# Last batch of an attention kernel: weight loads of the head behind the early gathers, value-weight splits on VectorE, first query tile ahead of the second's transposes

## What is computed

```python
x = x + xattn(layernorm(x), ctx)      # 16 heads of 32; text keys (118) and image keys (257),
                                      # each with its own softmax, the two outputs added, then @ o_w
h = layernorm(x)
score = h @ w_router                  # per token
idx = sort(top_k(score, 14))          # 14 tokens of every batch: 448 in all
sel = h[b, idx]
q, k, v = rms(sel) @ wq + bq, rms(sel) @ wk + bk, rms(sel) @ wv + bv   # 16 query, 8 key/value heads of 128
x1  = sel + causal_attention(rope(q), rope(k), v) @ wo
mlp = (silu(rms(x1) @ w_gate) * (rms(x1) @ w_up)) @ w_down
x = x + h.at[b, idx].set(gate * (x1 + mlp) + (1 - gate) * sel)        # gate = sigmoid(score)
```

## Time and profile before

| | us |
|---|---|
| median of 3 runs | 1636.01 (1633.88 to 1638.73) |
| the profiled execution | 1640.35, its span 1638.6 |
| PE (TensorE matmuls) busy | 1572.6, 96% of the span |
| DVE (VectorE) | 1195.5, 73% |
| ACT (ScalarE) | 708.7, 43% |
| POOL (GpSimd) | 703.5, 43% |
| DMA engines, mean over the span | 69 GB/s |

### The profile page before, as it was taken

One profiled execution on the slowest core, in us unless ns is written; L12 is line 12 of the kernel. 1 busy time (PEld: TensorE's weight loads), 2 busy tenths in 40 slices (PEclk: granted clock), 3 DMA queues, 4 the chain that ended last, 5 costly groups with the idle time before them and its releaser, 6 DMA issues.

```text
span 1638.6 us, 42293 instructions
## 1 busy us (share of the span) xinstructions
PE 1572.6 (96%) x16778; PEld 1219.5 (74%) x16778; DVE 1195.5 (73%) x1872; ACT 708.7 (43%) x1461; POOL 703.5 (43%) x781
## 2 busy tenths in 40 slices
PE   6999999999999999999999999999986999998997
PEld 5776777777777777777777777777765786777996
DVE  5753788877887788887888878788776685544775
ACT  5763444434444444444444444444434114555331
POOL 6761444344343444434444344443435581113552
PEclk9999999999999999999999999999996998999998
DMA  5842111112111121111211112111135223010000
GB/s 182 243 141 72 45 54 53 47 60 71 51 52 47 54 74 53 52 47 50 75 56 52 47 49 75 58 52 47 47 103 207 72 105 153 28 50 27 1 0 23
DMA packets 66167, 113.71 MB, mean 69 GB/s; under 512 B 21392, under 2 KB 36080, under 8 KB 64576
## 3 DMA queue, kind: packets, MB, share of 16 engines
q1 hardware_dynamic: 65280, 110.20, 21.4%
q0 software_dynamic: 832, 2.75, 0.5%
HBM read 82.59 MB, written 30.34 MB: 69 GB/s over the span
## 4 chain that ended last, share of the span: by engine, by line
PE 88%; ACT 5%; DVE 3%; DMA 2%; POOL 1%; issue 1%; SPq 0%; DVEq 0%; ACTq 0%; POOLq 0%
PE ps L1409 21%; PE ps L1410 18%; PE ps L1411 18%; PE ps L1539 7%; PE ps L1514 7%; PE ps L1487 3%; PE ps L1461 3%; PE ps L1724 2%; PE ps L1741 2%; ACT prob L770 2%; PE ps L1517 2%; PE ps L1733 1%; DMA xh_sel<-xh_dram,tok 1%; ACT prob L768 1%; PE ps L1443 1%
## 5 line engine op out<-in xcount | busy, mean ns | idle before, releaser
L490 POOL TENSOR_TENSOR ctx_lo<-ctx_raw,ctx_hi 128x472 fp32r<-128x472 f32 x64 | 115.4, 1827 | 310.6 <-ACT ctx_hi L711 310.6
L527 POOL TENSOR_TENSOR prob_img<-prob 128x448 f32<-128x448 f32 x128 | 160.3, 1253 | 189.2 <-ACT prob L770 189.1
L1075 DVE RECIPROCAL rec<-ps 128x224 f32<-128x224 f32 x128 | 199.0, 1555 | 6.8 <-PE ps L1539 3.2
L768 ACT ACTIVATE prob<-ps 119x448 f32<-119x448 f32 x128 | 69.7, 545 | 205.5 <-PE ps L1517 205.5
L1514 PEld LDWEIGHTS ps<-q_all,k_all 32*128 32x128 f32 (+1 forms) x3072 | 121.7, 186 | 49.3 <-issue 31.4
L1514 PE MATMUL ps<-q_all,k_all 32*128 32x112 f32 (+1 forms) x3072 | 148.3, 301 | 10.0 <-ACT prob L770 10.0
L1064 DVE TENSOR_REDUCE top<-ps 112x4 f32<-112x1028 f32 x128 | 156.2, 1221 | 0.0
L744 ACT ACTIVATE sq_junk<-proj 128x513 bf16<-128x513 f32 (+1 forms) x96 | 61.1, 637 | 172.5 <-DVE proj L1043 172.5
L1063 DVE TENSOR_REDUCE top<-ps 112x4 f32<-112x472 f32 x128 | 83.0, 649 | 65.8 <-PE ps L1487 65.8
L1069 DVE SCALAR_TENSOR_TENSOR prob_img<-prob,ones_last,prob_img 23x448 f32<-23x448 f32 x128 | 93.1, 727 | 42.6 <-POOL prob_img L527 39.5
L770 ACT ACTIVATE prob<-ps 128x896 f32<-128x896 f32 x128 | 116.9, 914 | 0.0
(11 more groups left out here) (326 smaller groups left out, 4421.3 us busy)
## 6 DMA issues: line engine op xcount, KB each, us to landing
ctx_raw<-in_ctx_dram SPq DMA_DIRECT2D x32, 748.0 KB, 4.2
xh_dram<-xh SPq DMA_DIRECT2D x32, 448.0 KB, 3.1
q_dram<-q_turned SPq DMA_DIRECT2D x28, 256.0 KB, 2.8
q_all<-q_dram SPq DMA_DIRECT2D x32, 224.0 KB, 3.1
xh<-in_x_dram SPq DMA_DIRECT2D x32, 224.0 KB
out_dram<-out_sb SPq DMA_DIRECT2D x32, 224.0 KB, 2.3
xa<-in_x_dram SPq DMA_DIRECT2D x21, 256.0 KB, 3.6
ring<-in_wq_dram SPq DMA_DIRECT2D x1, 4096.0 KB, 19.4
```

The costliest lines, as they stand in the source:

```text
L490: nc.gpsimd.tensor_tensor(ctx_lo[:, :, cols], ctx_raw[:, :, cols], ctx_hi[:, :, cols].bitcast(F32), ALU.subtract).then_inc(ctx_lo_done, 1)
L527: nc.gpsimd.tensor_tensor(prob_img[:, g % 2], prob[:, g % 2, 1, :], prob[:, g % 2, 2, :], ALU.add).then_inc(img_summed, 1)
L1075: nc.vector.reciprocal(rec[:], bank[:, 2:4]).then_inc(norm_step, 1)
```

## The change

Five edits:

1. SP, `last`: before the load of wq it waits for the three early gathers to have landed.
2. GpSimd, `last`: the three gathers are issued in one go right after `normalise_h(p)`, ahead of `output(p)` and `sum_image(i, 0)`. Three of the four value-weight splits leave GpSimd; the fourth (half 1, part 1) stays at the end and waits for all `oT_lo` parts of batch 31.
3. ScalarE, `last`: both `value_weights_hi` move up, from between the exponentials to just after `value_text(i)`, ahead of `turn_top(i, 0)`. VectorE, `last`: splits (0, 0), (0, 1) and (1, 0) run right after `score(p)`.
4. GpSimd behind the batches: `weights_lo(2)` waits until the normalised fourth chunk is written.
5. TensorE, prologue: `queries(0)` runs before `turn_x(1)`; from tile 1 on the order is as before.

```diff
@@ sync, last
                 sp.dma_start(xh[:, 0], t["x"][bass.ds(i, 1)].rearrange("o t d -> t (o d)")).then_inc(xres_loaded, 16)
+                for c in range(EARLY):
+                    sp.wait_ge(gathered[c], 16)
                 sp.dma_start(wq, t["wq"].rearrange("(c p) n -> p c n", p=P)).then_inc(ring_loaded[0], 16)
@@ gpsimd, last
                 normalise_h(p)
-                output(p)
                 pool.wait_ge(tok_ready, 1)
                 pool.wait_ge(xh_stored, 16 * EARLY_B)
                 pool.wait_ge(scaled, 3 * i + 3)
                 pool.wait_ge(k_tail_done, i + 1)
-                gather(0)
+                for c in range(EARLY):
+                    gather(c)
+                output(p)
                 sum_image(i, 0)
-                gather(1)
-                gather(2)
-                value_weights_lo(0, 0)
                 sum_image(i, 1)
-                value_weights_lo(0, 1)
                 sum_image(i, 2)
                 token_roots(slice(0, EARLY), 1)
                 sum_image(i, 3)
                 residual(i)
-                value_weights_lo(1, 0)
-                value_weights_lo(1, 1)
+                pool.wait_ge(oT_lo_done, B - 1 + KC)
+                at = (slice(None), slice(2, 4), slice(512, 1024))
+                nc.gpsimd.tensor_tensor(wv_lo[at], wv[at], wv_hi[at].bitcast(F32), ALU.subtract).then_inc(w_lo_done, 1)
@@ gpsimd, behind the batches
             token_roots(slice(EARLY, NC), 2)
+            pool.wait_ge(normed_ready, NC)
             weights_lo(2)
@@ scalar, last
                 value_text(i)
+                value_weights_hi(0)
+                value_weights_hi(1)
                 turn_top(i, 0)
                 turn_top(i, 1)
                 exps(i, 0)
-                value_weights_hi(0)
                 exps(i, 1)
-                value_weights_hi(1)
                 token_squares(0)
@@ vector, last
+            def value_weights_lo(half, part):
+                dve.wait_ge(w_hi_done, half + 1)
+                at = (slice(None), slice(2 * part, 2 * part + 2), slice(512 * half, 512 * half + 512))
+                return nc.vector.tensor_tensor(wv_lo[at], wv[at], wv_hi[at].bitcast(F32), ALU.subtract)
+
                 score(p)
+                value_weights_lo(0, 0)
+                value_weights_lo(0, 1)
+                value_weights_lo(1, 0).then_inc(w_lo_done, 1)
                 add_tail(i, 0)
@@ tensor, pre
                 turn_x(0)
+                queries(0)
+                turn_x(1)
                 for k in range(NT):
-                    if k + 1 < NT:
-                        turn_x(k + 1)
-                    queries(k)
                     if k:
+                        if k + 1 < NT:
+                            turn_x(k + 1)
+                        queries(k)
                         turn_q(k - 1)
```

## The result

| | before | after |
|---|---|---|
| median, runs on one chip | 1635.34 (4 runs, 1633.88 to 1638.73) | 1625.17 (4 runs, 1624.15 to 1627.08) |
| ratio, 95% interval | | 0.9936 [0.9918, 0.9955] |
| profiled execution | 1640.35, span 1638.6 | 1627.08, span 1625.3 |

The kernel is 10.2 us faster by medians and 13.3 us by spans; the forecast was 1622.7 in a range of 1617 to 1630. For the stages I use two quantities that need no absolute time. The **lead** is when the load of wv goes out (1213.04 before). The **stretch** runs from there to the first matmul of the head: 1290.54 - 1213.04 = 77.5 us before. After, it is 1277.21 - 1212.83 = 64.4 us. So 13.1 of the 13.3 us lie in the stretch and 0.2 in the lead.

What follows compares the result with a forecast made beforehand. TensorE matmuls, busy 96% of the span, bound the kernel, with waits in the last batch on gathers and one VectorE instruction. Gains 6.8 + 4.4 + 0.9 + 1.2 = 13.3 us off 1636.0 give 1622.7, range 1617 to 1630.

Steps and rivals of the forecast that it cites:

- Part 1: Last batch: gathers ahead of GpSimd's other work, with wq and wk loads behind them, gain 6.8 us.
- The cover of the roundings: ScalarE, last batch: moved roundings put topT(0) at 1225.0 instead of 1220.6; 0.4 us of cover, nothing on the path.
- Part 2: Last batch: moving value-weight splits off GpSimd cuts add_tail(3) from 6.29 to about 1.9 us, gain 4.4.
- Clock: TensorE: fewer gaps may keep it at 2.4 GHz in places, between nothing and 2 us; counted as nothing.
- Part 3: Behind the batches: GpSimd's wait before weights_lo(2) removes TensorE's idle time for normed_last, gain 0.9 us.
- Part 4: Prologue: running queries of x tile 0 first starts the batches earlier, gain 1.2 us, ends 0 and 2.2.
- the median is 4.3 below that execution; taken off the median: Final sum: the 13.3 us gain is subtracted from the median 1636.0, not the profiled 1640.35, giving 1622.7.
- A: Last batch: gathers and splits exclude each other, 3.3 us less gain, 1626.0 us; chance 0.15.
- B: Last batch: gathers are slow by themselves, not through wq; total gain 8.0 us, 1628.0; chance 0.06.
- C: Last batch: ScalarE's new wait for wv makes it slower than before, 1642 if wv takes 28 us; chance 0.04.
- D: Last batch and behind: wq's landing or the fourth gather holds what moved forward, half the gain, 1629; chance 0.07.

Runs made afterwards that it cites:

- e4: Kernel before with only the value-weight splits moved to VectorE and the roundings moved up; median 1636.80 us, ratio 1.0004.
- e3: Kernel before with only SP's wait for the three early gathers added ahead of wq and wk; median 1633.74 us, ratio 0.9985.
- e12: Changed kernel with all four value-weight splits back on GpSimd at their old places; median 1633.86 us, ratio 0.9975.
- e1: Kernel before with only the prologue edit, queries of x tile 0 ahead of tile 1's transposes; median 1635.35 us, ratio 1.0004.
- e6: Changed kernel without GpSimd's wait in front of weights_lo(2); median 1626.34 us, ratio 0.9932.
- e10: Changed kernel with GpSimd's old order of gathers, output and image sum, loads' wait kept; median 1625.26 us, ratio 0.9926.
- e8: e7 with residual(i) moved between the sums over images 1 and 2 on GpSimd; median 1621.21 us.
- e9: e7 with two GpSimd waits, before the batch's second image sum and before residual, that open gaps; median 1620.12 us, ratio 0.9901.
- e2: Changed kernel with the prologue's old order, without queries(0) first; median 1626.30 us, ratio 0.9942.
- e7: Changed kernel with GpSimd's first context split made in two parts, tiles 24 and 26 instead of 23; median 1622.41 us, ratio 0.9911.

## Why the prediction was right, point by point

**Part 1, right in its sum, partly by luck.** From wv's issue to exps(3) it is 27.3 us instead of 34.1: 6.8, the forecast's number. The gathers landed in 4.4 to 7.2 us (forecast 4.4 each). The terms inside were off. The forecast had exps(2) 7.4 us earlier and then 0.6 lost up to exps(3); measured are 6.2 and another 0.6 gained. Exps(2) started at 1236.46 and not 1235.3, because add_tail(0) took 1.54 us and not 0.68: I had put sum_image(0) in front of it and missed that sum_image(1) now follows without a gap and keeps VectorE out. The same 1 us came back further on: scores_T(3) started at 1238.87 and not 1238.1 (1.0 late, with the lead of 0.2), but its matmuls ran in 1.2 us instead of 2.1, at a granted clock of 1.00 instead of 0.50 (windows view, first before, then after):

```profile
1244.20:1246.50 2.30, 2.23 (x40) 2.12 (x44) 1.81 (x2) 0.21 (x2) 1.13 (x1) 0.50 1.00 367
```

```profile
1238.80:1240.10 1.30, 1.30 (x48) 1.17 (x44) 1.09 (x1) 0.00 (x0) 1.13 (x3) 1.00 0.96 391
```

The forecast had taken nothing for the clock, so two errors of 1 us cancelled. And wq went out at 1236.27 instead of 1233.8; it landed after 13.7 us, at 1250.0, within the 1253.2 of the forecast. The cover of the roundings held: topT(0) at 1224.08, wv landed after 7.6.

**Part 2, right in size; the partition between parts 1 and 2 is wrong.** From exps(3) to the end of add_tail(3) it was 8.9 us and is 4.7: 4.2, against 4.4, and e4 has the same by itself (4.3 us, a gain of 4.6). But the forecast gave the splits no other value and gave part 1 its full 6.8 by itself, and e3, e4 and e12 show otherwise. With the splits on GpSimd, shielding the gathers is worth 2.8 us (e3; e12, which has part 3 as well, comes to 2.9); with the gathers unshielded, moving the splits is worth 1.5; both together, and the 1.0 of part 3 set aside, 77.5 - 64.4 - 1.0 = 12.1. Some 8 us exist only for the pair, and nearly all of it lies ahead of exps(3): there the pair gains 6.8, while e3 gains 3.2, because VectorE is kept out, and e4 loses 3.7, because its splits hold up the gathers' issue. The times agree in kind: 2.5 us by e3's ratio, nothing by e4's, 10.5 by the changed kernel's, part 3 included. The row that shows the first half was in the trace of before, o_space with 3.16 us under the gathers' wait, and I had not priced what that wait was hiding.

**Clock.** Between the end of add_tail(3) and add_residual(31) another 1.0 us went (7.9 to 6.9). The forecast took 0 out of 0 to 2. The granted clock there was 0.50 in the earlier trace rows. In the changed kernel and, second, in e1 this stretch reads:

```profile
1244.80:1251.70 6.90, 6.30 (x72) 4.96 (x72) 6.09 (x12) 2.21 (x6) 1.21 (x1) 0.83 1.01 418
```

```profile
1255.40:1262.00 6.60, 5.99 (x30) 4.43 (x31) 5.95 (x11) 2.43 (x6) 0.00 (x0) 0.68 0.00 0
```

e1 took 6.6 us here without any edit of the last batch, so I don't count this 1.0 as the change's for certain. With the 0.9 in scores_T(3) the clock gave back 1.9 us in this one execution, the upper end of what the forecast allowed and took nothing for.

**Part 3, right.** 0.9 forecast, 1.0 in e6; normed_last 0.48 us.

**Part 4, the step that failed.** The 1.2 us were there at turn_q(0), as forecast, and are 0.2 at wv's issue, and nothing in the means over ten kernels. "Behind it the loop is again TensorE's own, so 1.0 to 1.5 stays" was wrong. TensorE waits 2.4 us at tile 23 in both kernels; the lead outlived even that, and was then spent at the lower clock. The 2.4 us stood in the trace of before; the fall of the clock did not.

**From the trace to the median.** By spans the forecast's 13.3 us is what came, with part 4 short by 1.0 and the clock's 1.0 in its place. That the sum agrees to the tenth is luck: the errors cancelled, and each span is one execution. By medians it is 10.2, inside an interval of 7.4 to 13.4 (1635.34 times 0.0045 and 0.0082). The difference is in the step "the median is 4.3 below that execution; taken off the median": the changed kernel's profiled execution stands only 1.9 above its median. In the profiled executions of these 14 kernels the part behind the first head matmul, the same program in all, took 343.5 to 348.1 us, and in before and after it happened to be the longest, 348.1 in both. Inside it, the attention stage from its first to its last maximum (neg_top on VectorE) took 126.8 to 127.7 us in seven of them, after included (127.4), and 128.4 to 129.2 in the other seven, before included (129.2); TensorE's granted clock was 0.99 over that stage in after and 0.96 in before. The part from there to the last result rows gave it back, 149.5 us in after and 147.5 in before. What decides this was not settled, and with it stays open where the 3 us between spans and medians went.

**Rivals.** A (1626.0) is nearer to the median, 1625.17, than the forecast's 1622.7 and can't be told from it by the time, but by the trace: no engine lost a whole turn. The second gather took 1.73 us beside the splits and 0.94 in e12 where VectorE was idle; the first gather of e4 and e10 took 1.96 beside a split and 1.19 in e3 without; the first gather of the changed kernel took 1.56 beside a split and 1.57 in e12 without. So splits cost a gather between nothing and 0.8 us, not its turn. By the Trainium skill, "SBUF — State Buffer", section "Who interferes with whom", arithmetic with two SBUF inputs on VectorE and a GpSimd instruction that reads SBUF block each other; the trace agrees for arithmetic. Its inference that such an instruction leaves descriptor generation alone is borne out for one of these three gathers and not quite for the other two, by 0.8 us each. B is out: 4.4 to 7.2 us of landing. C did not occur. D names something late behind the batch, and TensorE was busy 25.00 of 25 us there.

## What to carry to other kernels

Two waits that overlap hide each other: before pricing the removal of one, list every instruction in its shadow that takes longer than its usual time, since that is what will be late next. Where GpSimd and VectorE share the path, and a VectorE operation starts behind the first instruction of a GpSimd row without a gap, it is what is left of the row that counts here, not the instruction that happens to run; moving an instruction within the row moves the block, a gap ends it. And a lead won early has to be followed to each later idle time of the engine, with the granted clock beside it.

## What was not expected of the hardware

- A VectorE operation that started behind the first of several GpSimd instructions without a gap was not let in between them: 6.13 us for an operation of 0.68 us behind three (e12), 4.50 us for one of 0.27 behind three (e3), 2.10 for one of 0.27 behind two (e8). A gap of 0.8 us let it in at once (e9). All of these VectorE operations read two operands in SBUF.
- It is not so when VectorE starts first. add_tail(2) of the changed kernel started at 1241.52, 0.03 us ahead of sum_image(3), and ended at 1243.17, between sum_image(3) (1242.69) and the end of residual, which followed without a gap and took 1.67 us instead of 1.27; e2, e6, e7 and e12 show the same. It still took 1.65 us instead of 0.68.
- The other way round GpSimd was let in: output(p) of e4 started 0.17 us behind the first of VectorE's three splits in a row, took 2.17 us instead of 1.27, and ended before the second split did, which took 2.29 instead of 1.22 (e10 the same).
- Equal idle times of TensorE, 2.43 and 2.41 us, were followed by a granted clock of 1.00 in before and of 0.73 and 0.50 in after; up to there TensorE's program differs only in the order of the first two tiles, and the idle time began 1.5 us earlier. Over ten kernels it went the same way each time; why is not shown.
- Gathers of 112 rows of 4 KB landed in 4.4 to 7.2 us with wq held back and in up to 16.0 us beside it; wq in turn landed in 12.6 to 15.1 us behind them and in 19.4 to 20.6 beside them (before, e1, e4).
